# A vision block on one Trainium2 core: the second query tile's attention output on three PSUM banks, and the FFN's last sum moved behind the mixing's second scaling

## The reference

```
h  = LN(sigmoid(q) * (ew @ (exp(k)*v)) / (ew @ exp(k)) @ out_w + out_b + x)   # token mixer, 256 tokens x 256
h  = concat(cls_tok, h)                                                        # 257 tokens
z  = _layernorm(h);  q, k, v = z @ w_qkv                                       # 16 heads of 64
attn = softmax(q k^T * scale);  attn = einsum('bhij,hg->bgij', attn, reattn_w) # heads mixed
attn = (attn - mean_g) * rsqrt(var_g + 1e-3) * gamma + beta                    # normalised over the 16 heads
h  = h + (attn @ v) @ w_out + b_out
h  = h + bitlinear(silu(bitlinear(z2, w_gate)) * bitlinear(z2, w_up), w_down)  # z2 = _layernorm(h), inner 1024
```

## Time and profile before

| | |
|---|---|
| device time, median of 3 runs | 833.09 us (826.8 to 837.37) |
| the profiled execution's own time | 825.0 us |
| its span, first to last instruction | 823.2 us |
| TensorE busy | 673.1 us (82%) |
| VectorE busy | 564.5 us (69%) |
| ScalarE busy | 434.3 us (53%) |
| GpSimd busy | 212.0 us (26%) |
| mean granted TensorE clock | 0.955 |

### The profile page before, as it was taken

How to read it: one execution, slowest core, us unless ns; L and a number is a source line. 1 busy time by engine, 2 the same in 40 slices (tenths; PEclk the granted TensorE clock), 3 DMA queues, 4 the chain that set the end, 5 groups by cost and what they waited for, 6 DMA issues and landing times.

```text
span 823.2 us, 18887 instructions
## 1 busy us (share of the span) xinstructions
PE 673.1 (82%) x7618; PEld 472.2 (57%) x7634; DVE 564.5 (69%) x1215; ACT 434.3 (53%) x1230; POOL 212.0 (26%) x399
## 2 busy tenths in 40 slices
PE   0849758898789888998799868988799788966894
PEld 0536444766467655766467645766476656743552
DVE  0596638666875689567966779567956696656755
ACT  0103716484575737483647547482748365754722
POOL 0307224202540153112520254014410353003300
PEclk9969978999999999999999999999999999998997
DMA  8400560036201451056103621155104700353000
GB/s 324 169 1 3 175 239 22 1 130 226 81 18 54 158 207 35 2 168 249 34 2 113 222 85 35 34 172 213 34 2 154 259 14 2 90 204 129 6 1 14
DMA packets 42395, 83.98 MB, mean 102 GB/s; under 512 B 3003, under 2 KB 6596, under 8 KB 41668
## 3 DMA queue, kind: packets, MB, share of 16 engines
q1 hardware_dynamic: 41268, 79.29, 28.0%
q10 hardware_dynamic: 1040, 3.49, 1.1%
HBM read 46.98 MB, written 35.79 MB: 101 GB/s over the span
## 4 chain that ended last, share of the span: by engine, by line
PE 41%; DVE 24%; DMA 15%; ACT 11%; issue 6%; POOL 2%; SPq 0%; POOLq 0%; ACTq 0%; DVEq 0%
DMA pg<-turned 9%; PE big L568 7%; PE small L568 7%; PE big L585 7%; DMA turned<-pst 6%; PE small L729 5%; DVE var L1330 5%; DVE an L1374 4%; ACT pst L1001 3%; PE small L714 3%; ACT ot L1089 2%; PE big L662 2%; DVE mx L1295 1%; ACT sqb L1021 1%; PE small L684 1%
## 5 line engine op out<-in xcount | busy, mean ns | idle before, releaser
L1001 ACT ACTIVATE pst<-big,nb 128x256 f32<-128x256 f32 x256 | 117.9, 474 | 32.0 <-DVE nb L1298 32.0
L1295 DVE TENSOR_REDUCE mx<-big 128x4 f32<-128x1024 f32 x64 | 78.3, 1223 | 52.4 <-PE big L585 51.7
L662 PEld LDWEIGHTS big<-pst,pg 64*64 64x64 f32 x4096 | 67.9, 140 | 52.7 <-DVE an L1374 31.7
L662 PE MATMUL big<-pst,pg 64*64 64x64 f32 x4096 | 75.2, 227 | 23.8 <-DVE an L1374 14.3
L1021 ACT ACTIVATE sqb<-big 128x1024 f32<-128x1024 f32 x64 | 65.1, 1019 | 31.1 <-PE big L662 29.6
L1374 DVE TENSOR_TENSOR an<-big,rstd 128x1024 f32<-128x1024 f32 x64 | 78.3, 1224 | 2.2
L1330 DVE TENSOR_REDUCE var<-sqb 128x64 f32<-128x1024 f32 x64 | 77.3, 1210 | 2.2 <-ACT sqb L1021 2.2
L585 PE MATMUL big<-qk_t 64*128 64x256 f32 x512 | 72.6, 402 | 3.8 <-ACT qk_t L984 3.7
L714 PE MATMUL small<-an,v 128*64 128x130 f32 (+1 forms) x768 | 55.5, 285 | 21.2 <-ACT ot L1089 20.5
L684 PE MATMUL small<-w_qkv,xnv 128*128 128x512 f32 x128 | 64.9, 630 | 8.3 <-DVE h L1476 5.6
L568 PE MATMUL small<-xnt,w_qkv 128*128 128x256 f32 x256 | 63.8, 392 | 0.0
(11 more groups left out here) (210 smaller groups left out, 1244.9 us busy)
## 6 DMA issues: line engine op xcount, KB each, us to landing
turned<-pst SPq DMA_DIRECT2D x128, 257.0 KB
pg<-turned SPq DMA_DIRECT2D x16, 2056.0 KB, 11.0
w_qkv<-in_w_qkv SPq DMA_DIRECT2D x1, 3072.0 KB
xt<-in_x_t SPq DMA_DIRECT2D x8, 256.0 KB, 2.9
xr<-in_x_tok SPq DMA_DIRECT2D x8, 256.0 KB, 2.8
out<-h SPq DMA_DIRECT2D x16, 128.0 KB
an<-in_gate_t ACTq DMA_DIRECT2D x1, 1024.0 KB, 7.5
an<-in_up_t ACTq DMA_DIRECT2D x1, 1024.0 KB, 10.2
```

The source lines that it names most:

```text
L662: last = mm(mix_place(n)[half[0]:half[1], k_hi * 512 + i * 64:k_hi * 512 + (i + 1) * 64], pg[rows, ib, j], w_rows[rows, it, ib, :], start= ...
L1001: last = A(pst[:, g % 2, h % GH, it * T:(it + 1) * T], big[p % 2][:, (j * TT + it) * T:(j * TT + it + 1) * T], ACT.Exp, bias=nb[:, h, it:i ...
L1295: V.reduce_max(mx[:, hs, :], big[p % 2][:, :].rearrange("p (h t l) -> p h t l", h=2, t=TT), AX)\
```

## The change

The parts of the second query tile's attention use banks 3, 0, 1, 3 in every image but the last, where they stay at 3, 0, 3, 0. Part 2, now on bank 1, waits for VectorE's read of the second `mixer_kv` product there (("kv", 1)) and not for ScalarE's copy of part 0. Part 3, now on bank 3, waits for the copy of part 0, and not for that of part 1. `mixer_q` moves ahead of part 3. The wait of `mixer_sums` is as it was. On VectorE `ffn_out(b - 1, ff, P, 1)` moves from behind variance(2) to behind the scaling of group 1. No instruction is added or removed, and no DMA is moved.

```diff
-        def o_bank(it, g):
-            return bank[(3, 2)[g % 2] if it == 0 else (3, 0)[g % 2]]
+        def o_bank(b, it, g):
+            if it == 0:
+                return bank[(3, 2)[g % 2]]
+            return bank[((3, 0, 3, 0) if is_(b, B - 1) else (3, 0, 1, 3))[g]]
...
-                if it == 1 and g == 1 and not is_(b, B - 1) and not is_(b, B - 2):
-                    pe.wait_ge(dve_a.sem, dve_a.at(b + 2, ("kv", 0)))
+                if it == 1 and g in (1, 2) and not is_(b, B - 1) and not is_(b, B - 2):
+                    pe.wait_ge(dve_a.sem, dve_a.at(b + 2, ("kv", g - 1)))
...
-                if g >= 2:
+                if g >= 2 and (it == 0 or is_(b, B - 1)):
                     pe.wait_ge(act_o.sem, act_o.at(b, ("o", it, g - 2)))
+                elif g == 3:
+                    pe.wait_ge(act_o.sem, act_o.at(b, ("o", it, 0)))
...
                 attend(b, 1, 2)
+                if do_mixer:
+                    mixer_q(b + 2)
                 attend(b, 1, 3)
                 if do_mixer:
-                    mixer_q(b + 2)
                     mixer_sums(b + 2)
...
-                    if n == 1:
-                        if not is_(b, 0):
-                            ffn_out(b - 1, ff, P, 1)
-                    elif n == 5:
+                    if n == 5:
                         class_parts()
...
                     elif n == 1:
+                        if not is_(b, 0):
+                            ffn_out(b - 1, ff, P, 1)
                         dve.wait_ge(act_r.sem, act_r.at(b, "qs"))
```

More of the change, by code:

```diff
@@ L713, in attend @@
                         for jt in range(TT):
-                            last = mm(o_bank(it, g)[j * DH:(j + 1) * DH, q * T:q * T + n],
+                            last = mm(o_bank(b, it, g)[j * DH:(j + 1) * DH, q * T:q * T + n],
                                       v[:, jt, h * DH:(h + 1) * DH], an[:, jt, h // 2, cols, h % 2],
@@ L1080, in attend @@
                         p = 2 * g + q
-                        last = A(obias[:, p:p + 1], o_bank(it, g)[:, q * T + ONE:q * T + ONE + 1], ACT.Copy,
+                        last = A(obias[:, p:p + 1], o_bank(b, it, g)[:, q * T + ONE:q * T + ONE + 1], ACT.Copy,
                                  scale=beta[:, p:p + 1])
@@ L1088, in attend @@
                     p = 2 * g + q
-                    last = A(ot[:, p, dst], o_bank(it, g)[:, q * T:q * T + n], ACT.Identity, bias=obias[:, p:p + 1],
+                    last = A(ot[:, p, dst], o_bank(b, it, g)[:, q * T:q * T + n], ACT.Identity, bias=obias[:, p:p + 1],
                              scale=gamma[:, p:p + 1])
```

## The result

| | before | changed |
|---|---|---|
| device time, median | 830.09 us (826.8 to 837.37, 4 runs) | 844.42 us (840.08 to 847.52, 4 runs) |
| ratio | | 1.0158, 95% interval 1.0113 to 1.0202 |
| the profiled execution's own time | 825.0 us | 840.08 us |
| its span | 823.2 us | 838.3 us |
| mean granted TensorE clock | 0.955 | 0.941 |

The kernel is slower, by 9.4 to 16.8 us on 830.09; the forecast sum was 7.3 us. A fourth run has moved the median of the kernel before from 833.09 to 830.09 us, on which the same sum gives 837.4 and not 840.4. Whether the loss is more than 2% can't be told, since the interval ends at 2.02%.

What follows compares the result with a forecast made beforehand. Bound by a chain through TensorE in the scores, mostly the HBM gather in the window behind them, then engine hops to VectorE's class parts. -1.3 + 8.6 = +7.3 us on 833.09 gave 840.4, forecast as 840, range 830 to 849.

Steps and rivals of the forecast that it cites:

- the forecast sum: Whole kernel: -1.3 us for the three banks and +8.6 us for the later `ffn_out`, together +7.3 us.
- the first rival: TensorE's longer wait before `values(b, 0, 1)` brings the lower clock: 2.1 us a stage, 848 if four are hit; chance 0.17.
- the forecast path: Mixing stage: later `ffn_out` delays TensorE's values, ScalarE's copy and square(4), then VectorE up to the class parts, 1.4 us.
- In most passes: Ahead of `values(b, 0, 1)`: TensorE's wait for `ffn_out` would be about 2.3 us in most passes, for 0.76.
- Part one, three banks, -1.3 us: Window of the second query tile's attention: 1.1 us gained in the first full pass, 0.2 in the second, nothing elsewhere.
- The new wait ahead of `mixer_sums`: TensorE behind the second tile's attention: with `mixer_q`'s cover gone, about 0.9 us waiting for ScalarE's copy of part 3.
- Part two, 1.4 us a regular stage: `ffn_out` behind group 1's scaling: five regular mixing stages 1.4 us longer, +0.1 and +1.5 in two others, +8.6 us.
- The stage at 488 us, +0.1: Mixing stage with a late down product: the scaling fits into VectorE's 1.19 us wait, class parts only 0.1 us later.
- The third rival: Mixing stage: unseen slack in the values' copy or ScalarE's order absorbs the delay, leaving 832 us; chance 0.13.
- the second, TensorE late throughout: TensorE ends the windows, down products come late: banks gain 7 x 1.0, `ffn_out` costs 7 x 0.1, 827 us; chance 0.10.

Runs made afterwards that it cites:

- the further delay: Changed kernel with the FFN's last sum (`ffn_out`) moved once more, behind the scaling of group 2: 868.6 us, ratio 1.0427 to the kernel before.
- the split wait: Changed kernel with the wait of `mixer_sums` split, first half for bank 0's copy, second for bank 1's: 846.47 us, ratio 1.0163 to the kernel before.

## Why the prediction was right, and where its size was off

The direction and the mechanism of the delay were right, and the time lies in the range. The sum does not explain it: it holds half of the loss. The other half is the first rival, which had a chance of 0.17 and is what happened beside the forecast path. The range held both together: it was wide for a spread between executions that no row explained, and it took in the near part of that rival. That the time lies in it does not confirm the sum, and this part of the hit is luck.

The steps of the path are in the trace where the working put them: the scaling starts at 0.26 us behind rstd and `ffn_out` 1.14 us behind that, TensorE's wait is 2.33 us (predicted 2.3) in three stages and 2.89 in the last, VectorE waits ahead of the sums of squares of groups 4 and 5 (0.50 and 0.24 us in the pass at 581 us, the values at 1.98), and the further delay passed through about one to one. "In most passes" was too much for the 2.3 us: in three of seven TensorE waited only 1.24 or 1.42, since the lower clock had made it late.

- **Part one, three banks, -1.3 us: not contradicted, but not measured so finely.** The new wait ahead of `mixer_sums` is 0.99 us, for 0.9. The profiled windows gave 1.0 us, but not where the working had it: 0.7 in the first (for 1.1), nothing in the second (for 0.2), and 0.9 in the fourth, counted as nothing, where the gather's piece of the chain was 13.27 us for the 14.16 of the earlier trace rows, while the other four changed by 0.3 or less. With the banks alone the timed runs gave 0.3 to 6.5 us. That nothing is left to gain there was shown by the split wait.
- **Part two, 1.4 us a regular stage: a little small.** It is 1.57 us at the full clock. The 1.4 us are there at rstd(4); of the rest, the mixer's two norm rows behind group 4 took 0.89 us for 0.75; I had them unchanged, and no run tried why.
- **The stage at 488 us, +0.1: wrong.** The step "five are regular, in one the down product came late" took a property of one execution for one of the program. The lower clock that had made the product late was elsewhere in the next execution. The stage took 26.58 us, as long as the first, third and sixth, and cost 2.0 us over its own 24.58.
- **The first rival: mis-set, 0.17.** "The longer wait brings the lower clock" is what happened: the values were long in five of seven stages, behind waits of 1.42 us once and 2.33 to 2.89 in the others. The price was 1.5 us a stage, not 2.1. The 2.1 had both the values and group 4 slow from end to end; in the trace the lower clock lasts for less than both, and where group 4 was slow too (1.99 us) the values took only 2.73. The mistake is in the words against it, "six of seven don't": that row was read at a stall of 0.76 us and was no evidence on one of 2.33. The forecast's 840 should have carried 5 x 1.5 = 7.5 us more; with it the sum is 14.8 us, for 13.1 by the ratio, 14.3 by the medians and 15.1 by the profiled spans.

The third rival, slack that I didn't see, fell with the further delay; the second, TensorE late throughout, with the split wait.

The Trainium skill, TensorE: Matmul & The Clock Gate, section Why this matters for your kernels, warns of idle gaps between bursts of matmuls, but only of longer ones than the stalls in the changed kernel. The trace goes further than that: the values took 2.73 to 3.68 us behind the three stalls of 2.33 us in the changed kernel, and 1.98 where spare work stood in them. Here the measurement decides.

## What to carry to other kernels

Ask of a moved instruction who takes its result, not whether its engine has work to do meanwhile: VectorE lost nothing by doing the big scaling first, but the small sum released a bank, and behind that bank stood one engine's queue and then the next one's. Where a wait is taken away in front of work that is hidden beside a transfer, look first at what the transfer's taker waits for. And a stall on TensorE's queue has a second price behind it, the clock of the next matmuls: price it from rows at the lower clock for the new length of the stall, not from how seldom the old one paid it.

## What the runs showed of the hardware

In the kernels with the sum moved once, TensorE came to the stall at the full clock (the down product at 1.05 us) and stood 2.33 to 3.06 us with nothing in the stall in 15 stages. The values then took 2.41 to 3.78 us for 1.98 in 13 of them; the two exceptions (behind 2.46 and 2.99 us) are in the kernel with the split wait. With spare matmuls in such a stall it was none of 10. Where the clock had fallen before the stall, TensorE stood 0.91 to 1.53 us, and the values were long in two of nine stages. With the sum moved twice, at stalls of 3.5 to 5.6 us, it was seven of seven. Where the sum was not moved and the stalls were 0.58 to 1.5 us it was one of 35. So the length of the stall matters, and does not settle a single case.

What I had not expected is that a time of matmuls that compute nothing, 1.28 us in a stall of 2.3, is enough to keep the values at 1.98 us. Ahead of group 3 three such matmuls (0.89 us) did not always hold the clock: in two of 18 stages that have them group 3 still took 1.98 or 1.99 us. The clock fell at group 3 or the down product in 22 of 49 stages of the kernels with the sum moved and in 5 of 35 of the others, though the wait ahead of group 3 is mostly the same 1.07 us; no run tried why. The clock's place varies between executions of nearly the same program, so one profile doesn't tell which stage pays.
